# Routing of a mixture of experts: the end of attention laid flat, four buffers for the exps, choices in three parts

## The reference, cut to what matters

```python
h = tok(x, position)                       # 4096 tokens x 128, each a mean over 10 embeddings
h = h + attention(layernorm(h))            # 16 sequences x 256 tokens, 8 heads of 64, causal
def ffn(x):                                # x = layernorm(h), 4096 x 128
    probs = softmax(x @ router_w + router_b)       # 64 experts
    top_w, top_idx = top_k(probs, 42)
    top_w = softmax(top_w)                         # a second softmax, over the 42 chosen
    comb = zeros((N, 64)).at[rows, top_idx].set(top_w)
    h = gelu(einsum('td,edh->teh', x, w1) + b1)    # every expert for every token, 256 hidden
    y = einsum('teh,ehd->ted', h, w2) + b2
    return einsum('ted,te->td', y, comb)
return h + ffn(layernorm(h))
```

## Time and profile before

| | |
|---|---|
| median of three runs | 1905.59 us |
| the profiled execution, its own time | 1909.42 us |
| its span (first to last instruction) | 1907.6 us |
| mean granted clock of TensorE | 0.968 |
| PE busy | 1784.0 us, 94% |
| DVE busy | 1566.6 us, 82% |
| ACT busy | 1530.4 us, 80% |
| POOL busy | 1410.9 us, 74% |
| first product of the experts | 494.5 us |

### The profile page before, as it was taken

How to read it: one execution, slowest core, us unless ns; L and a number is a source line. 1 busy time by engine, 2 the same in 40 slices (tenths; PEclk the granted TensorE clock), 3 DMA queues, 4 the chain that set the end, 5 groups by cost and what they waited for, 6 DMA issues and landing times.

```text
span 1907.6 us, 29977 instructions
## 1 busy us (share of the span) xinstructions
PE 1784.0 (94%) x8423; PEld 1428.7 (75%) x8423; DVE 1566.6 (82%) x2194; ACT 1530.4 (80%) x2733; POOL 1410.9 (74%) x837
## 2 busy tenths in 40 slices
PE   5469699997899999999999999999999999999998
PEld 3445466665688888888888888888888888888886
DVE  7649788886588888888888888888888888888887
ACT  2258688886888888888888888888888888888886
POOL 4343076654298898888888888688888888888886
PEclk9977799997799999999999999999999999999999
DMA  7410000001533333333333333333333333333332
GB/s 219 138 46 18 1 1 0 0 4 34 122 123 126 111 130 122 114 126 125 114 132 116 112 135 110 111 138 110 120 128 110 134 113 113 135 110 126 121 110 66
DMA packets 107016, 191.86 MB, mean 101 GB/s; under 512 B 13750, under 2 KB 86438, under 8 KB 90790
## 3 DMA queue, kind: packets, MB, share of 16 engines
q1 hardware_dynamic: 104894, 186.77, 29.1%
q0 software_dynamic: 2048, 4.20, 0.7%
HBM read 179.40 MB, written 11.53 MB: 100 GB/s over the span
## 4 chain that ended last, share of the span: by engine, by line
PE 75%; DVE 6%; ACT 4%; issue 2%; POOL 2%; POOLq 0%; DVEq 0%; ACTq 0%
PE f_ps_h L2259 12%; PE f_ps_h L2261 12%; PE f_ps_h L2260 12%; PE f_ps_y L2272 12%; PE f_ps_y L2273 12%; PE f_ps_y L2274 12%; PE ps_s L1482 2%; PE ps_ko L1468 2%; DVE neg_max L1372 1%; POOL y_sum L2113 1%; DVE q_t L1341 1%; ACT p_t L1250 1%; PE ps_p L1435 1%; DVE g_lo L2213 1%; DVE sm L1365 1%
## 5 line engine op out<-in xcount | busy, mean ns | idle before, releaser
L2113 POOL TENSOR_TENSOR y_sum<-y_sum,weighed 128x512 f32<-128x512 f32 x504 | 1028.6, 2052 | 101.6 <-DVE weighed L2205 94.5
L2213 DVE TENSOR_TENSOR g_lo<-gelu_out,g_hi 128x1024 fp32r<-128x1024 f32 x512 | 815.8, 1593 | 86.5 <-ACT g_hi L2154 70.2
L2145 ACT ACTIVATE gelu_out<-f_ps_h,b_t 128x512 f32<-128x512 f32 x1024 | 649.6, 686 | 193.7 <-PE f_ps_h L2261 191.4
L2154 ACT ACTIVATE g_hi<-gelu_out 128x1024 fp32r<-128x1024 f32 x512 | 542.0, 1059 | 0.0
L2205 DVE SCALAR_TENSOR_TENSOR weighed<-f_ps_y,b_t,c_row 128x512 f32<-128x512 f32 x504 | 375.6, 745 | 119.7 <-PE f_ps_y L2274 118.6
L2272 PE MATMUL f_ps_y<-g_hi,w_hi 128*128 128x512 f32 x1024 | 400.0, 391 | 3.2 <-DVE g_lo L2213 2.5
L2259 PE MATMUL f_ps_h<-x_hi,w_hi 128*128 128x512 f32 x1024 | 399.8, 390 | 2.6 <-ACT e L1685 2.6
L2260 PE MATMUL f_ps_h<-x_lo,w_hi 128*128 128x512 f32 x1024 | 399.4, 390 | 0.0
L2261 PE MATMUL f_ps_h<-x_hi,w_lo 128*128 128x512 f32 x1024 | 399.4, 390 | 0.0
L2273 PE MATMUL f_ps_y<-g_lo,w_hi 128*128 128x512 f32 x1024 | 398.5, 389 | 0.0
L2274 PE MATMUL f_ps_y<-g_hi,w_lo 128*128 128x512 f32 x1024 | 398.5, 389 | 0.0
(11 more groups left out here) (228 smaller groups left out, 1564.7 us busy)
## 6 DMA issues: line engine op xcount, KB each, us to landing
c_row<-comb_rows SPq DMA_DIRECT2D x124, 1024.0 KB, 4.9
w_raw<-in_w SPq DMA_DIRECT2D x256, 128.0 KB, 4.4
c_row<-comb_rows SPq DMA_DIRECT2D x16, 256.0 KB, 5.6
by_slot<-b_zeros SPq DMA_DIRECT2D x1, 3072.0 KB, 13.2
b_gauss_s<-by_slot SPq DMA_DIRECT2D x12, 256.0 KB, 5.5
mixed_rows<-mixed SPq DMA_DIRECT2D x12, 256.0 KB, 2.2
out<-h SPq DMA_DIRECT2D x8, 256.0 KB, 4.8
cent<-in_centers SPq DMA_DIRECT2D x1, 1536.0 KB
```

The lines of the kernel that those rows point to most:

```text
L2113: pool.tensor_tensor(y_sum[:, w, g, :], y_sum[:, w, g, :], weighed[:, r % 2, :], ALU.add).then_inc(added, 1)
L2145: last = act.activation(gelu_out[:, r % GELUS, c, :], ps_h[:, r % 2, c, :], ACT.Gelu, bias=b_t[:, c, bass.ds(e, 1)])
L2154: act.activation(g_hi[:, r % RING], gelu_out[:, r % GELUS], ACT.Copy).then_inc(hi_ready, 1)
L2213: dve.tensor_tensor(g_lo[:, r % RING], gelu_out[:, r % GELUS], g_hi[:, r % RING].bitcast(F32), ALU.subtract).then_inc(lo_ready, 1)
```

## The change

It has six parts.

1. `all_steps` ends after step 33. What steps 34 to 36 held is written out flat, per engine: no part of it is padded to a step.
2. All norms of the routing move to GpSimd (before: quads 0 to 2 on ScalarE). `root` part 0 on ScalarE now stands behind `copy_p` of unit 30, and `root` part 1 moves from behind `second_exps(3)` to the end of attention's block.
3. `neg_p` and `e2` of the early quads get four buffers each instead of two, and `probabilities` waits for `exp_two` at q-1 for every q.
4. The choices of quads 0 and 1 leave attention's block. In `route` a choice is cut: quad 0 in three parts (2, 2 and 3 rounds with the end), quads 1 and 2 in two (4 rounds; 3 rounds with the end), each put between a `maximum` and the next `probabilities`, or behind the last `probabilities`; quad 3 comes whole at the very end.
5. ScalarE's `weigh` and `copy_comb` of the early quads come later in its order. `weigh(2)` is its last routing instruction.
6. `turn_comb` of quads 2 and 3 goes into the experts' steps 1 and 4 on TensorE (ahead of `first(1)` and of `second(0)`), `copy_comb(2)`, `weigh(3)` and `copy_comb(3)` into steps 0 and 2 on ScalarE.

The diff, cut to its core:

```diff
@@ attend
-            for u in range(UNITS - 4, UNITS + 5):
+            for u in range(UNITS - 4, UNITS + 2):
                 step(u, u % 4)
@@ attend, scalar (what step() held for the router at u = 33, 34, 35 is gone)
             all_steps(act, step)
+            copy_p(EVEN, EVEN % 4, 0)
+            router.root(act, 0)
+            router.warm_exp(act)
+            copy_p(ODD, ODD % 4, 0)
+            copy_p(ODD, ODD % 4, 1)
+            router.copy_x(act, 0)
+            router.first_exps(act, 0)
+            router.copy_x(act, 1)
+            router.second_exps(act, 0)
             router.first_exps(act, 1)
+            copy_mv(UNITS - 4)
             router.copy_x(act, 2)
-            router.second_exps(act, 1)
-            router.first_exps(act, 2)
-            router.copy_x(act, 3)
-            copy_mv(UNITS - 4)
+            router.root(act, 1)
+            router.warm_exp(act)
@@ attend, vector
             all_steps(dve, step)
+            copy_o(EVEN - 1)
+            last_of(EVEN - 1)
+            router.deviations(dve, 0)
+            copy_o(EVEN)
+            last_of(EVEN)
+            router.maximum(dve, 0)
+            router.probabilities(dve, 0)
+            copy_o(ODD)
+            router.maximum(dve, 1)
+            last_of(ODD)
@@ attend, tensor
             all_steps(pe, step)
+            turn_p(EVEN, EVEN % 4, 0)
+            project_out(EVEN - 1)
+            mix(EVEN, EVEN % 4)
+            turn_p(ODD, ODD % 4, 0)
+            project_out(EVEN)
+            turn_p(ODD, ODD % 4, 1)
+            pe.wait_ge(masked, UNITS)
+            router.turn_x(pe, 0)
+            router.logit(pe, 0)
+            mix(ODD, ODD % 4)
+            router.turn_x(pe, 1)
+            router.logit(pe, 1)
+            project_out(ODD)
@@ routing
-    neg_p_early = sb("neg_p", [P, 2, QT, EXPERTS])
-    e2_early = sb("e2", [P, 2, QT, EXPERTS])
+    neg_p_early = sb("neg_p", [P, EARLY, QT, EXPERTS])
+    e2_early = sb("e2", [P, EARLY, QT, EXPERTS])
@@ route, scalar (new order, whole)
+        second_exps(1) first_exps(2) copy_x(3) second_exps(2) first_exps(3) copy_x(4)
+        second_exps(3) weigh(0) first_exps(4) copy_x(5) second_exps(4) copy_comb(0)
+        first_exps(5) copy_x(6) second_exps(5) weigh(1) first_exps(6) copy_x(7)
+        second_exps(6) copy_comb(1) first_exps(7) second_exps(7) weigh(2)
@@ route, gpsimd (new order, whole)
+        norm(0) norm(1); for q in 2..7: norm(q), low_x(q - 2), and for q = 6, 7 the split of
+        an expert's weights; low_x(6) low_x(7)
@@ route, vector (new order, whole; "choose q a:b" are rounds a to b-1, "rest" has the end)
+        probabilities(1); wait mv_copied; shifted_of(1) maximum(2) choose 0 0:2 deviations(1)
+        probabilities(2) maximum(3) choose 0 2:4 probabilities(3) maximum(4) choose 0 rest
+        copy_b1 probabilities(4) maximum(5) choose 1 0:4 probabilities(5) maximum(6)
+        choose 1 rest probabilities(6) maximum(7) choose 2 0:4 probabilities(7)
+        choose 2 rest, choose 3 whole
@@ route, tensor (new order, whole)
+        turn_x(2) logit(2) turn_b1 turn_x(3) logit(3) turn_x(4) logit(4) turn_x(5)
+        turn_comb(0) logit(5) turn_x(6) logit(6) turn_x(7); wait b1_copied; turn_comb(1) logit(7)
@@ experts, scalar
                 gelu(S, e, r)
+                if isinstance(S, int) and S == 0:
+                    router.copy_comb(act, EARLY - 2)
+                if isinstance(S, int) and S == 2:
+                    router.weigh(act, EARLY - 1)
...
                 high(S - 1, (r - 1) % BODY)
+                if isinstance(S, int) and S == 2:
+                    router.copy_comb(act, EARLY - 1)
@@ experts, tensor
                 for r in range(BODY):
+                    if w == 0 and r == 1:
+                        router.turn_comb(pe, EARLY - 2)
+                    if w == 0 and r == LAG:
+                        router.turn_comb(pe, EARLY - 1)
```

More of the change, by code:

```diff
@@ L1334, in _ @@
             all_steps(pool, step)
+            step(UNITS + 2, 2)
         @block.vector
@@ L1648, in root, with norm @@
         act.activation(root_of[:, PART_TILES[part]], shifted[:, PART_TILES[part]], ACT.Sqrt).then_inc(rooted, 1)
[L1650 to L1660, removed]
+    def norm(pool, q):
         pool.wait_ge(ln_ready, 2 if q == QUADS - 1 else 1)
-        pool.wait_ge(turned, q - 1)
+        after(pool, turned, q - 1)
         for k in range(QT):
@@ L1666, in norm_late @@
                                       ALU.add)
[L1667 removed]
+        last.then_inc(normed, 1)
     def warm_exp(act):
[L1670 removed]
+        act.activation(warm[:], ident[:, 0:1], ACT.Exp, scale=0.0)
     def copy_x(act, q):
@@ L1780, in choose_end, with choose_part, choose_rest @@
         dve.reciprocal(r2[:, b], s2[:]).then_inc(r2_ready, 1)
-    def choose(dve, q):
-        for n in range(len(ROUNDS_OF_CHOICE)):
+    def choose_part(dve, q, first, last):
+        for n in range(first, last):
             choose_round(dve, q, n)
+    def choose_rest(dve, q, first):
+        choose_part(dve, q, first, len(ROUNDS_OF_CHOICE))
         choose_end(dve, q)
@@ L1831, in turn_comb @@
             last.then_inc(comb_turned, 1)
-    return Routing(load_router, root, norm, norm_late, warm_exp, copy_x, first_exps, second_exps, weigh, copy_comb,
-                   low_x, shifted_of, deviations, maximum, probabilities, choose, choose_round, choose_end, copy_b1, turn_x, logit, turn_b1, turn_comb,
+    return Routing(load_router, root, norm, warm_exp, copy_x, first_exps, second_exps, weigh, copy_comb,
+                   low_x, shifted_of, deviations, maximum, probabilities, choose_part, choose_rest, choose_round,
+                   choose_end, copy_b1, turn_x, logit, turn_b1, turn_comb,
                    hi_ready, x_used, exp_one, b1_copied, comb_copied)
@@ L1859, in _ @@
     def _(act):
-        router.weigh(act, 0)
+        router.second_exps(act, 1)
+        router.first_exps(act, 2)
+        router.copy_x(act, 3)
         router.second_exps(act, 2)
@@ L1877, in _ @@
-        router.weigh(act, 3)
         router.second_exps(act, 5)
+        router.weigh(act, 1)
+        router.first_exps(act, 6)
         router.copy_x(act, 7)
-        router.first_exps(act, 6)
-        router.copy_comb(act, 3)
         router.second_exps(act, 6)
+        router.copy_comb(act, 1)
         router.first_exps(act, 7)
         router.second_exps(act, 7)
+        router.weigh(act, 2)
     @block.gpsimd
     def _(pool):
[L1888 to L1895, removed]
+        router.norm(pool, 0)
@@ L1896, in _ @@
+        router.norm(pool, 1)
+        for q in range(2, QUADS):
+            router.norm(pool, q)
+            router.low_x(pool, q - 2)
+            if QUADS - SPLIT_EARLY <= q:
+                r = q - (QUADS - SPLIT_EARLY)
                 round_weights(pool, f, r, r, 32)
                 rest_of_weights(pool, f, r, f["hi_copied"], r + 1)
+        router.low_x(pool, QUADS - 2)
+        router.low_x(pool, QUADS - 1)
     @block.vector
     def _(dve):
+        router.probabilities(dve, 1)
+        dve.wait_ge(mv_copied, TILES // 4)
@@ L1901, in _ @@
+        router.shifted_of(dve, 1)
         router.maximum(dve, 2)
-        router.copy_b1(dve)
+        router.choose_part(dve, 0, 0, 2)
+        router.deviations(dve, 1)
         router.probabilities(dve, 2)
         router.maximum(dve, 3)
-        router.choose(dve, 2)
+        router.choose_part(dve, 0, 2, 4)
         router.probabilities(dve, 3)
-        dve.wait_ge(mv_copied, TILES // 4)
-        router.shifted_of(dve, 1)
         router.maximum(dve, 4)
[L1910 to L1915, removed]
@@ L1916, in _ @@
-        router.choose_end(dve, 3)
+        router.choose_rest(dve, 0, 4)
+        router.copy_b1(dve)
+        router.probabilities(dve, 4)
+        router.maximum(dve, 5)
+        router.choose_part(dve, 1, 0, 4)
         router.probabilities(dve, 5)
         router.maximum(dve, 6)
+        router.choose_rest(dve, 1, 4)
         router.probabilities(dve, 6)
         router.maximum(dve, 7)
+        router.choose_part(dve, 2, 0, 4)
         router.probabilities(dve, 7)
+        router.choose_rest(dve, 2, 4)
```

76 lines of the change are left out of this document (17 added, 59 removed).

## The result

The changed kernel takes 1906.49 us (median of 22 runs, 1903.43 to 1910.32), against 1903.32 us for the kernel before in the same runs (22, 1897.72 to 1906.62). The ratio is 1.0020, with a 95% interval of 1.0013 to 1.0027, which is 2.5 to 5.1 us slower (3.8 by the ratio, 3.2 by the two medians) and stands clear of the measurement. The forecast was 1906.0 within 1901.4 to 1911.4, and +0.4 us against the kernel before. The median lay 0.5 from the forecast by luck: the change itself cost 2.8 to 3.4 more than forecast, and the kernel before, measured again, came out 2.3 us lower than in its first three runs.

The account below looks back on a forecast made before the run. Experts keep TensorE busy without a gap, so only the instant of second(0) could move; before it, chains of waits bind. -0.4, +0.3 and +0.5 give +0.4 us on 1905.6, so 1906.0, range 1901.4 to 1911.4.

Parts of the forecast that it names:

- Attention's tail: End of attention, at the high clock: copy_p(30) no longer behind root; attention ends some 6 us sooner, quad 1 3 us ahead.
- rival C: Attention's tail from 441 us: TensorE falls to 1.2 GHz through waits, costing 4.4 us, total 1910.4; chance 0.15.
- The quads: Routing quads 3 to 7: 4.3 to 4.4 us each without a choice, but ScalarE waits at weigh(0) and weigh(1).
- B: Routing: closer-packed quads give TensorE the high clock, saving 5.4 us, total 1900.6; chance 0.12.
- D: Routing: cut choices fit beside the other engines, exps 4 start up to 3.5 us sooner, total 1902.5; chance 0.08.
- The give-back: Experts' first steps: start 5.5 us sooner, but late choices, weighs and turnings put second(0) at 503.9 against 504.31, -0.4 us.
- The fourth row: Experts near second(5): the fourth row group lands near 515.8, with second(5) wanted at 517.5; +0.3 us, bounds 0 and +2.7.
- The +0.5 for handovers and for VectorE beside GpSimd: About ten new handovers placed without latency, and VectorE beside GpSimd at new places: +0.5 us, bounds -1.5 and +2.
- The sum: Whole kernel: -0.4 for second(0), +0.3 for late rows, +0.5 for what no row shows, together +0.4 us.

Follow-up runs that it names:

- e3_later: Changed kernel with weigh(0), weigh(1) behind copy_x(5), copy_x(7) on ScalarE and turn_comb(0), turn_comb(1) behind logit(5), logit(7) on TensorE; 1908.38 us, 1.0005 of the kernel before.
- e2_before_rows: Kernel before the change, with the first round's rows loaded by expert, one row piece of expert 0 per quad; 1908.28 us, ratio 0.9998.
- e7_root_early: Changed kernel with root part 0 and its warm-up ahead of copy_p(30); 1911.0 us in one run, against 1908.99 for the kernel before.
- e8_all_root: Changed kernel with rows by expert, weighs 0, 1, 3 and turnings later, root part 1 behind copy_x(3), second_exps(1), (2) behind copy_x(4); 0.9949 of the kernel before.

## Why the prediction was right, point by point

**Attention's tail.** Right to 0.2 us, and to 0.4 at the first product. Predicted from `turn_p(30)` at 436.82: `logit(0)` 8.9 behind it, `mix(31)` at 10.0, `logit(1)` 13.3, first product 52.2. Measured: 8.87, 9.90, 13.11, 52.57. The clock was 1.00 in 440 to 450, which excludes rival C here: the gap before projection 30 was 0.53 us. By the Trainium skill's rule on turnings (TensorE: Matmul & The Clock Gate, Part 4: PE-mode transpose) the tail would have run low; it did not: eight turnings took 1.09 us in it, where eight at the low clock took 1.92 before.

**The quads.** Right in mechanism and nearly in size: ScalarE stands before `weigh(0)` for 3.61 us, before `weigh(1)` for 1.84, where about 3 was forecast for each. The clock is 0.50 from 465 to 490, so B is out; the exps of quad 4 start 33.25 after `turn_p(30)`, where I had 33.7 and D up to 3.5 less, so D is out too. e3_later shows that these orders, and not an engine's load, cost 7.6 us.

**The give-back.** Right: `second(0)` forecast at 67.1 after `turn_p(30)`, measured 67.06, and 66.48 in the second profile. The 5.1 us by which the experts start sooner are gone at `weigh(2)`, `turn_comb(2)` (a wait of 2.64) and `turn_comb(3)` (1.54).

**The fourth row.** The right wait in the right place, and far too small: +0.3 with an upper bound of 2.7, measured +4.3. Two parts were mis-sized. The rows were issued 5.96 us after `second(0)`, where I placed 4.1 within 3.1 to 6.1, and had landed 8.4 behind that, where I took 7.5 to 8: 14.34 after `second(0)` in place of 11.9, so 2.4 later. With the 0.3 this is the 2.6 that the wait cost, just inside the bound. The other 1.7 I had not priced at all: behind the wait nine products ran at 1.2 GHz. That such a wait can bring it was to be read from the row of 441.90, low after a wait of 1.80, which I used against rival C and not here. It doesn't always: the same products after the same 1.80 ran at the high clock in e2_before_rows, and those after 1.73 at `second(5)` did in e7_root_early.

```profile
445.23 1.08 PE L1468 MATMUL ps_ko<-p_t,v_s 128*64 128x512 f32 x4 [1.80 <-ACT p_t L1250]
```

**The +0.5 for handovers and for VectorE beside GpSimd.** Not there at `second(0)`: the chain of estimates held without it. The meeting itself was there, `neg_s` of quad 5 with its 1.20 us; `maximum(6)` came 0.3 later than placed, and the estimates behind it had room for that.

**The sum.** -0.4 and +4.3 give +3.9, within the interval of the measured +2.5 to +5.1. Forecast was +0.4, "same" at 0.67 and "slower" at 0.16. The measured ratio is at the very bound of 0.2% between the two. So the account up to `second(0)` was right, the price of the late rows was not, and the median near 1906.0 is no proof of the sum.

## What to carry to other kernels

Moving work to start the next stage sooner gives nothing until the first instruction that must then run without a break comes sooner: compute that instant, and every transfer that it newly runs into. A stage that starts earlier meets transfers that don't. Here a small write that had to be confirmed waited for the large loads ahead of it in its queue; sending first only the piece that the first step needs took that away. Two edits that gave 1 to 3 us each gave 9.5 to 11 together, so take away one bound before you judge the other.

## What the runs showed of the hardware that I had not expected

- After one and the same wait of 2.42 us before `turn_p(29)`'s second block, TensorE ran eight turnings at the high clock in three profiles (1.09 us: e2_before_rows, e7_root_early, e8_all_root) and at the low clock, wholly or in part, in the other seven (1.46 to 1.97). The waits at `second(5)` were followed by the low clock at 2.44, 3.04 and 5.46 us, and by the high one at 1.73.
- Unchanged code ahead of `turn_p(30)` took from 432.98 to 440.06 us in ten profiles, more than most edits here are worth. Profiles were comparable only from a common instant onwards.
- A write of one quad's weights (128 KB) took 2.25 to 2.3 us with nothing in its queue. Given while 1 MB of row loads was under way it took 5.00 in the changed kernel, 5.74 in its second profile, and 4.3 to 8.2 in e3_later and the kernel before.
